# One-hots transposed by a DMA, ScalarE's work reordered, and an edited start, in a fused conv, cluster and blend kernel on one core

## The reference

```python
xn = x / max(norm(x, axis=1), EPS)             # x: (8, 512, 32, 48), f32
cn = centroids / max(norm(centroids), EPS)     # 40 x 512
idx = argmax(einsum('bchw,nc->bnhw', xn, cn), axis=1)
onehot = one_hot(idx, 40)
sum_x = einsum('bhwn,bchw->bnc', onehot, x)    # cluster sums of each image
count = sum(onehot, axis=(1, 2))
centroids_local = sum_x / max(count, 1)[..., None]
delta = centroids_local[b, idx] - x
alpha = exp(-mean(delta * delta, axis=1))
y = x + alpha * delta
out = relu(einsum('oc,bchw->bohw', W, y) + b)  # W: 512 x 512
```

## Time and profile before

| | |
|---|---|
| median of 3 runs | 420.41 us (419.93 to 420.76) |
| the profiled execution | 420.21 us |
| its span, first to last instruction | 418.4 us |
| PE busy | 410.1 us, 98% |
| DVE busy | 335.4 us, 80% |
| ACT busy | 256.0 us, 61% |
| POOL busy | 257.7 us, 62% |
| chain that ended last | 95% PE |
| mean DMA rate | 177 GB/s |

### The profile page before, as it was taken

The page is one execution under the profiler, slowest core; times in us unless marked ns, Lnnn a source line. Parts: engine busy times, 40 slices in busy tenths (PEclk is TensorE's granted clock), DMA queues, the critical chain, the costliest instruction groups (busy, mean ns, idle before and its releaser), DMA issues.

```text
span 418.4 us, 5854 instructions
## 1 busy us (share of the span) xinstructions
PE 410.1 (98%) x2123; PEld 291.6 (70%) x2146; DVE 335.4 (80%) x411; ACT 256.0 (61%) x351; POOL 257.7 (62%) x113
## 2 busy tenths in 40 slices
PE   8999999999999999999999999999999999999996
PEld 5744466775777767775867758776777758777885
DVE  1469969789789879899798888898798897798730
ACT  4765374766764675665855666746756658566641
POOL 2000654993599666993879936996769938334420
PEclk9999999999999999999999999999999999999999
DMA  7998295997389384966669572993847220222223
GB/s 265 320 289 149 47 254 157 294 254 200 103 222 282 109 223 136 273 169 184 216 164 259 180 203 101 251 252 126 217 137 226 100 102 1 102 100 100 97 78 128
DMA packets 71071, 73.94 MB, mean 177 GB/s; under 512 B 2868, under 2 KB 45876, under 8 KB 71044
## 3 DMA queue, kind: packets, MB, share of 16 engines
q1 hardware_dynamic: 71044, 73.58, 62.9%
HBM read 48.40 MB, written 25.17 MB: 176 GB/s over the span
## 4 chain that ended last, share of the span: by engine, by line
PE 95%; ACT 2%; DVE 1%; issue 1%; POOL 0%; POOLq 0%
PE main L897 21%; PE main L898 20%; PE main L899 20%; PE fa L790 10%; PE sump L839 9%; PE gat L872 5%; PE fa L814 1%; PE fa L799 1%; PE al L879 1%; PE main L940 1%; PE al L885 1%; PE gat L885 1%; PE al L919 1%; PE main L912 1%; ACT oht L631 1%
## 5 line engine op out<-in xcount | busy, mean ns | idle before, releaser
L897 PE MATMUL main<-yh,wh 128*128 128x512 f32 x376 | 152.7, 406 | 0.0
L898 PE MATMUL main<-yl,wh 128*128 128x512 f32 x376 | 146.7, 390 | 0.0
L899 PE MATMUL main<-yh,wl 128*128 128x512 f32 x376 | 146.7, 390 | 0.0
L316 POOL TENSOR_TENSOR z<-z,x 128x1024 f32<-128x1024 f32 x42 | 99.8, 2396 | 66.7 <-DVE z L443 66.7
L323 POOL TENSOR_TENSOR yl<-z,yh 128x1024 fp32r<-128x1024 f32 x44 | 105.6, 2418 | 55.6 <-ACT yh L600 55.6
L608 ACT ACTIVATE o<-main,bcol 128x512 f32<-128x512 f32 x96 | 65.3, 683 | 60.9 <-PE main L899 60.8
L897 PEld LDWEIGHTS main<-yh,wh 128*128 128x128 f32 x376 | 70.6, 188 | 21.0 <-issue 5.0
L899 PEld LDWEIGHTS main<-yh,wl 128*128 128x128 f32 x376 | 70.6, 188 | 15.2
L898 PEld LDWEIGHTS main<-yl,wh 128*128 128x128 f32 x376 | 70.7, 188 | 13.8
L330 POOL TENSOR_TENSOR xr<-xt 128x2048 f32<-128x2048 f32 x11 | 51.5, 4686 | 20.8 <-DVE xt L356 20.8
L419 DVE TENSOR_TENSOR z<-gat,x 128x1024 f32<-128x1024 f32 x46 | 56.2, 1223 | 8.3 <-PE gat L872 8.1
(11 more groups left out here) (118 smaller groups left out, 377.2 us busy)
## 6 DMA issues: line engine op xcount, KB each, us to landing
out<-o SPq DMA_DIRECT2D x23, 1024.0 KB, 7.3
x<-x SPq DMA_DIRECT2D x21, 1024.0 KB, 5.5
xs<-x SPq DMA_DIRECT2D x84, 256.0 KB, 5.6
x<-x SPq DMA_DIRECT2D x12, 256.0 KB, 5.3
o<-w SPq DMA_DIRECT2D x1, 1024.0 KB, 8.4
out<-o SPq DMA_DIRECT2D x4, 256.0 KB, 2.0
sq<-centroids SPq DMA_DIRECT2D x2, 80.0 KB
bcol<-bias SPq DMA_DIRECT2D x1, 2.0 KB, 8.3
```

The lines of the kernel that those rows point to most:

```text
L316: pool.tensor_tensor(z, z, X[g // PARTS % 2][:, pair(h), span(g)], ALU.add).then_inc(y_pool, 1)
L897: t_.matmul(main[:, o % 2, :], WH[:, k, rows], YH[g % 2][:, k, :], start=(k == 0), stop=False)
L898: t_.matmul(main[:, o % 2, :], WH[:, k, rows], YL[g % 2][:, k, :], start=False, stop=False)
L899: last = t_.matmul(main[:, o % 2, :], WL[:, k, rows], YH[g % 2][:, k, :], start=False, stop=(k == KC - 1))
```

## The change

What it does, in parts:

1. From batch 1 on the one-hots are transposed by a DMA (`dma_start_transpose`, SBUF to SBUF, issued by SP) into `ohT`; PE's 12 products for each of 7 batches go. SP waits for `oh3` before it, and the transposition stands behind `load_x(g+5)` and ahead of `load_xs(g+6)` in the batch's second unit. The DMA keeps the order of the tiles, so the similarities read their pixels in another grouping, `slot` becomes plain, and the gather's moving operand is read in 16 runs of 32 elements.
2. ACT no longer evacuates PSUM for these batches. Instead `count_onehot` copies `ohT` once more to a dead tile, for the counts alone. It waits for the DMA. `add_halves` no longer waits for `ohT_done`.
3. In the third unit of a batch ACT's order is changed: `relu(g-2, 0)` ahead of the second `high_half`, `relu(g-2, 1)` ahead of `high_sum`.
4. Start: POOL sets `ones` first, PE runs 5 idle products on `ones` (2 on the identity before) ahead of the centroids' transposition, and 2 (4 before) behind it. ACT runs a dummy exponential first. The second load of the centroids goes ahead of two of the first x blocks.
5. DVE in batch 0: `low_clusters(0)` ahead of the first `transpose_half(3, 0)`, and `transpose_half(3, 1)` later, behind `delta(0, 1)`.
6. SP waits for `cop_done` (the sums of batch 0 added) before `load_xs(4)`.

```diff
+        def wait_onehot(eng, b):
+            if b == 0:
+                eng.wait_ge(ohT_done, 1)
+            else:
+                eng.wait_ge(ohT_in, 16 * b)
...
+            def transpose_onehot(b):
+                sp.wait_ge(oh3_done, b + 1)
+                wait(sp, gat_done, 2 * PARTS * (b - 1))
+                sp.dma_start_transpose(ohT[b % 2][:, :].rearrange("n (s i) -> n s i", i=P),
+                                       oh3[:, :, :].rearrange("p s n -> p (s n)")).then_inc(ohT_in, 16)
...
-            load_x(0)
-            sp.dma_start(craw[column_tiles[1], :], cent).then_inc(c_in[1], 16)
-            load_x(1)
-            load_x(2)
+            for u in range(PARTS):
+                for k in range(KC):
+                    sp.dma_start(X[0][:, k, span(u)], x_rows[0, :, k, span(u)]).then_inc(first_in[u][k], 16)
+                    if (u, k) == (0, 1):
+                        sp.dma_start(craw[column_tiles[1], :], cent).then_inc(c_in[1], 16)
...
             load_x(5)
+            sp.wait_ge(cop_done, 1)
             load_xs(4)
             load_xs(5)
+            transpose_onehot(1)
             load_xs(6)
...
                     load_x(g + 5)
+                if g % PARTS == 1 and g // PARTS + 1 < BATCH:
+                    transpose_onehot(g // PARTS + 1)
                 if g + 6 < UNITS:
                     load_xs(g + 6)
...
             low_weights(1)
+            low_clusters(0)
             transpose_half(3, 0)
-            low_clusters(0)
-            transpose_half(3, 1)
             counts(0)
...
                 delta(g, 1)
+                if g == 0:
+                    transpose_half(3, 1)
...
+            def count_onehot(b):
+                wait_onehot(act, b)
+                act.wait_ge(simT_done, b + 1)
                 wait(act, g_ready, b)
-                wait(act, gat_done, 2 * PARTS * (b - 1))
-                a_.activation(ohT[b % 2][:, :], ohP[0:NK, 0:HW], ACT.Copy, accum_out=count[:, :]
-                              ).then_inc(ohT_done, 1)
+                a_.activation(simS[:, :, :, :].rearrange("p u t s -> p (u t s)").bitcast(BF16)[0:NK, 0:HW],
+                              ohT[b % 2][:, :], ACT.Copy, accum_out=count[:, :]).then_inc(ohT_done, 1)
...
+            act.wait_ge(cT_done, 1)
+            a_.activation(warm[:, :], cT[:, 0, N:N + 1], ACT.Exp).then_inc(warm_done, 1)
...
             high_half(0, 1)
+            count_onehot(1)
             high_half(1, 0)
...
                     copy_sums(b + 1)
-                    evacuate_onehot(b + 1)
+                    count_onehot(b + 1)
                     high_half(g - 1, 0)
                     square(g, 1)
+                    relu(g - 2, 0)
                     high_half(g - 1, 1)
-                    relu(g - 2, 0)
                     scale_means(b + 1)
                     move_upper(g)
                     high_means(b + 1)
+                    relu(g - 2, 1)
                     high_sum(g)
-                    relu(g - 2, 1)
...
             def add_halves(b):
-                if b > 0:
-                    pe.wait_ge(ohT_done, b + 1)
...
+                toks = ohT[b % 2][:, span(g)]
+                if not plain(b):
+                    toks = toks.rearrange("n (t q i) -> n q t i", t=TILES, q=Q)
...
+            pe.wait_ge(ones_done, 1)
+            keep_busy(5)
             pe.wait_ge(ident_done, 5)
-            keep_busy(2)
...
-            keep_busy(4)
+            keep_busy(2)
```

More of the change, by code:

```diff
@@ L289, in _ @@
         def _(pool):
+            pool.memset(ones[:, :].bitcast(F32), 1.0).then_inc(ones_done, 1)
             pool.memset(ident[:, :], 0.0).then_inc(ident_done, 1)
[L291 removed]
             pool.memset(select0, 0.0).then_inc(ident_done, 1)
@@ L622, in copy_onehot, with evacuate_onehot @@
                 act.wait_ge(oh_done, b + 1)
-                wait(act, ohP_done, b)
+                if b > 0:
+                    if b == 1:
+                        act.wait_ge(ohP_done, 1)
+                    else:
+                        act.wait_ge(ohT_in, 16 * (b - 1))
                 a_.activation(oh3[:, :, 0:USED].rearrange("p s (r n) -> p s r n", r=COPIES), oh[:, :, 0:N].unsqueeze(2).to_broadcast(
                     [P, PARTS * TILES, COPIES, N]), ACT.Copy).then_inc(oh3_done, 1)
-            def evacuate_onehot(b):
-                act.wait_ge(ohP_done, b + 1)
+            def evacuate_onehot():
+                act.wait_ge(ohP_done, 1)
+                a_.activation(ohT[0][:, :], ohP[0:NK, 0:HW], ACT.Copy, accum_out=count[:, :]
+                              ).then_inc(ohT_done, 1)
+            def count_onehot(b):
+                wait_onehot(act, b)
+                act.wait_ge(simT_done, b + 1)
                 wait(act, g_ready, b)
-                wait(act, gat_done, 2 * PARTS * (b - 1))
-                a_.activation(ohT[b % 2][:, :], ohP[0:NK, 0:HW], ACT.Copy, accum_out=count[:, :]
-                              ).then_inc(ohT_done, 1)
+                a_.activation(simS[:, :, :, :].rearrange("p u t s -> p (u t s)").bitcast(BF16)[0:NK, 0:HW],
+                              ohT[b % 2][:, :], ACT.Copy, accum_out=count[:, :]).then_inc(ohT_done, 1)
             def copy_sums(b):
@@ L802, in slot, with transpose_onehot @@
             def slot(u, t):
-                return (u * HALF + t % HALF) * 2 + t // HALF
-            def transpose_onehot(b):
-                pe.wait_ge(oh3_done, b + 1)
-                for u in range(PARTS):
-                    for t in range(TILES):
-                        dst = ohP[0:NK, u * UNIT:(u + 1) * UNIT]
-                        if plain(b):
-                            dst = dst[:, t * P:(t + 1) * P]
-                        else:
-                            dst = dst.rearrange("n (q t i) -> n q t i", q=Q, t=TILES)[:, :, t, :]
-                        last = t_.transpose(dst, oh3[:, slot(u, t), :], identb[:, :])
+                return u * TILES + t
+            def transpose_onehot():
+                pe.wait_ge(oh3_done, 1)
+                for s in range(PARTS * TILES):
+                    last = t_.transpose(ohP[0:NK, s * P:(s + 1) * P], oh3[:, s, :], identb[:, :])
                 last.then_inc(ohP_done, 1)
@@ L869, in gather @@
                     pe.wait_ge(s_done, folded(g - 1))
+                toks = ohT[b % 2][:, span(g)]
+                if not plain(b):
+                    toks = toks.rearrange("n (t q i) -> n q t i", t=TILES, q=Q)
                 for j in range(2):
                     k = 2 * h + j
-                    last = t_.matmul(banks(g, h)[:, j, :], G[:, k * P:(k + 1) * P], ohT[b % 2][:, span(g)],
-                                     start=True, stop=True)
+                    last = t_.matmul(banks(g, h)[:, j, :], G[:, k * P:(k + 1) * P], toks, start=True, stop=True)
                 last.then_inc(gat_done, 1)
@@ L918, in keep_busy @@
                 for _ in range(times):
-                    t_.matmul(al[:, 0:P], ident[:, :], ident[:, :], start=True, stop=True)
+                    t_.matmul(al[:, 0:P], ones[:, :].bitcast(F32), ones[:, :].bitcast(F32), start=True, stop=True)
+            pe.wait_ge(ones_done, 1)
+            keep_busy(5)
             pe.wait_ge(ident_done, 5)
-            keep_busy(2)
             pe.wait_ge(c_in[0], 16)
```

28 lines of the change are left out of this document (11 added, 17 removed).

## The result

The changed kernel takes 415.12 us (median, 414.26 to 415.43), the kernel before 420.31 us beside it: a ratio of 0.9873, with an interval of 0.9854 to 0.9891. The forecast was 414.8 us. The profiled execution has a span of 413.5 us, 4.9 us less than before.

A forecast was written before the change was run, and what follows sets the result against it. PE, busy 98% of the span, was taken to bound the steady part; at the start and in batch 1, PE, ACT and DVE wait in turn. 4.3 + 0.8 + 0.8 - 0.3 = 5.6 us off 420.4 gave 414.8 us, range 413.3 to 419.0.

The forecast's parts named there:

- Part 1: PE in batches 2 to 7: dropping 12 transposition products per batch saves 0.72 us each time, 4.3 us in all.
- Part 2: ACT's counting copy waits for the transposing DMA, taken as 4.6 us; PE feels it only over 6.2 us, so no cost.
- three bounds: Estimates of the transposing DMA's time from plain DMAs: 2.4 us below, 3.9 us in the middle, 5.7 us above.
- The reserve behind the window: Slack before PE feels a late counting copy, beyond ACT's 5.3 us window after oh3 is written: 0.9 us.
- the threshold: Time of the transposing DMA above which PE in the steady batches would be delayed: 6.2 us.
- The harsh form of the rival: Transposing DMA moves its 12 blocks one by one, 15.2 us; the kernel takes about 475 us; chance 0.03.
- Part 3: Gather products reading ohT in 16 runs of 32 elements: no cost; a doubling would cost 18 us, chance 0.02.
- Part 4: Batch 1, where PE waited: ACT's square and the rest of the chain to G come sooner, gaining 0.8 us.
- Part 5: Start: similarities begin sooner, gaining 0.8 us (0 to 1.3); DVE's new order in batch 0 loses 0.3 us (0 to 0.5).
- the start gives nothing: Rival at the kernel's start: x lands later than thought and the clock stays; 415.6 to 416.4 us, chance 0.12.
- x late: At the start, x lands later than the 7.5 us assumed; half of a rival of 415.6 to 416.4 us, chance 0.12.
- the clock stays: At the start, PE's clock rises no sooner; half of a rival of 415.6 to 416.4 us, chance 0.12.

## Why the prediction was right, step by step

- **Part 1, 4.3 us.** Measured 4.2: five periods of 0.74 and 0.50 in the first, where TensorE loses 0.2 to 0.3 us once at 77 us. With the products put back, all of it goes; with the relu order undone, 3.0 of it. The reading by distances, 0.95 - 0.22, was good to 0.02 us; the shown 0.83 us for twelve products would have given 5.0.
- **Part 2, nothing.** Right in its result, with two wrong sizes. The DMA takes 3.7 us where I took 4.6; of the three bounds the middle one, 3.9, was nearest. The reserve behind the window was 0.4 us, not 0.9, and the threshold about 5.6 us. With T at its taken value nothing would have been lost either, but the upper bound of 5.7 us lay just past the threshold, not 0.5 us short of it. That SP waits inside its queue cost nothing in the steady part, as taken: the only wait of TensorE for a DMA that the view shows is the one at 33.98 us. The harsh form of the rival did not come, for all twelve blocks land in 3.7 us. So the Trainium skill's 1309 ns for 128 x 128 (page "VectorE: DVE Perf Modes", section "The three transpose paths") can't be multiplied by the blocks. A second 384 KB side by side added 5.6 - 3.7 = 1.9 us, 207 GB/s. That is a fifth under the Trainium skill's 261 GB/s (page "DMA: Bandwidth & Descriptors", section "Latency and other measured facts"); for this transfer the measured figure counts.
- **The relu order** was counted as 0.6 us of that reserve. Its worth is 3.0 us of the 5.2, for 0.6 us misses the wait for POOL at `high_half`, which appears only once TensorE and ACT run ahead. I had no rival for that, since the change brought the edit along; that the sum comes out all the same is luck in this part. Someone who had made the DMA edit alone with this prediction in hand would have forecast 415 and measured 418.3.
- **Part 3.** Right, 384 ns.
- **Part 4, 0.8 us.** Right in place and size. `add_halves` waits for `sums_l`, as said, 2.61 us behind the gather in place of 2.91. To the first gather of unit 3 it is 4.65 us in place of 5.14 (its first product of two is missing in the earlier trace rows, 0.23 us ahead of the row shown). 0.30 + 0.49 = 0.79 us.
- **Part 5, +0.8 - 0.3.** The mis-sized term. At the gather of unit 2 the changed kernel is 0.18 us late (56.42 against 56.24), not 0.5 us early, and by the medians the start is worth nothing. The 0.47 us by which the similarities start sooner is near the 0.7 taken; but x landed later than the 7.5 us assumed, at 8.1, and 0.3 us is left when the sums start (20.48 against 20.79). Then 0.49 us goes between the gathers of unit 0 and unit 1, 0.42 of it as a wait for x of unit 5 (33.98 us), a term that the prediction did not have. In this trace that wait covers what DVE's new order costs: to the gather of unit 2 it is 20.56 us, as before, where traces without the wait show 0.3 us more. The edit that sends the centroids ahead of x likely gave back what idle products and exponential had won. The case stood among the rivals as "the start gives nothing", 415.6 to 416.4 us; of its mechanism "x late" was right in this trace, "the clock stays" was not: the last passes and the transposition of x ran faster than before.
- **The sum.** Spans: -0.2 to unit 2, 0.8 in batch 1, 4.2 in the steady part, 4.9 with the rounding, where 5.6 was forecast. The medians differ by 5.2 us, of which 0.3 us lies within the spread of either.

## What to carry to other kernels

Where one engine is full and the others keep up, a product taken from it is worth the distance between starts, and the gain arrives only as far as the next engine's order lets it: look, behind the freed place, for instructions that wait with ready work behind them, and price the reordering together with the edit that needs it. Here the DMA alone gave 2.1 us, the whole change 5.2, and the reordering nothing in the steady part while the products stayed. A load that is moved ahead of others may be paid by those that it passes; ask who reads it first.

## What the runs showed that I had not expected

- A transposition of 128 x 1536 bf16 from SBUF to SBUF occupied SP's queue for 1.44 us and landed after 3.7 us, seven times alike (3.7 to 3.8). Two of them side by side took 5.6 us, one behind the other 7.4 us.
- The landing of the first loads differs from one execution to another by more than most edits of the start are worth. Eight of the kernels share the code and the order of loads up to there (all but those with a changed start); in them the sums of batch 0 start between 19.69 us (two transpositions in a row) and 20.64 us (relu order undone), though the similarities start at 5.07 to 5.15 us in all. A single trace can't price an edit of the start to better than some 0.5 us.
- How soon TensorE's passes get faster at the start differs between executions of the same start. The granted clock reads 1.00 throughout there; the level is read from the distance of the passes, 0.21 us at the lower one (1.2 GHz) and 0.11 us at the upper (2.4 GHz). With the new start, no idle time ahead of the 16 passes and none in them, they took 2.84 us (DVE's old order) to 3.68 us (products put back); with the old one, again with no idle time, 2.65 us (DMA alone) to 3.68 us (kernel before). So the 3.68 us behind a gap of 0.59 us, in the kernel without the exponential, do not show that a gap keeps the clock down.
